# An interaction tower on one core: ScalarE's five banks per job added by GpSimd alone, or by an accumulating DMA and GpSimd

## What is computed

```python
prev = x.transpose(...)                       # [b, e, h], h = 39, then 128, 128
for k in range(3):
    z = einsum('bmd,bhd->bdmh', x, prev)      # 39 fields times h
    t = z.reshape(b, d, m*h) @ ws[k] + bs[k]  # to 128 units
    t = t / sqrt(sum(t*t over units and d))   # a norm per example
    logit.append(t); prev = t
features = sum(concatenate(logit), over d)    # 384 per example
```

## Time and profile before

| | |
|---|---|
| three timed runs | 1060.4, 1061.88, 1062.07 us (median 1061.88) |
| profiled execution | 1062.48 us, its span 1060.8 us |
| PE busy | 1028.2 us (97%) |
| DVE busy | 983.6 us (93%) |
| POOL busy | 865.9 us (82%) |
| ACT busy | 791.3 us (75%) |
| granted TensorE clock | 1.00 throughout |

### The profile page before, as it was taken

One profiled execution on the slowest core, in us unless ns is written; L12 is line 12 of the kernel. 1 busy time (PEld: TensorE's weight loads), 2 busy tenths in 40 slices (PEclk: granted clock), 3 DMA queues, 4 the chain that ended last, 5 costly groups with the idle time before them and its releaser, 6 DMA issues.

```text
span 1060.8 us, 17970 instructions
## 1 busy us (share of the span) xinstructions
PE 1028.2 (97%) x4320; PEld 782.4 (74%) x4320; DVE 983.6 (93%) x3344; ACT 791.3 (75%) x2655; POOL 865.9 (82%) x729
## 2 busy tenths in 40 slices
PE   2999999999999999999999999999999999999998
PEld 0477777878777787877778787777878777788884
DVE  2589999999999999999999999999999999999993
ACT  3476877868788786868778687777868778788872
POOL 6777988889898888988888898888889888577770
PEclk9999999999999999999999999999999999999999
DMA  5650030302303030120303012030301203000000
GB/s 188 129 143 12 3 88 3 89 2 52 96 4 88 3 87 4 21 71 2 89 3 87 5 28 64 3 89 2 85 7 17 74 3 89 1 1 1 2 1 1
DMA packets 75892, 46.10 MB, mean 43 GB/s; under 512 B 55689, under 2 KB 58633, under 8 KB 75658
## 3 DMA queue, kind: packets, MB, share of 16 engines
q1 hardware_dynamic: 68487, 38.59, 15.2%
q10 hardware_dynamic: 2179, 5.07, 1.4%
q0 software_dynamic: 5120, 1.29, 1.4%
HBM read 42.99 MB, written 1.94 MB: 42 GB/s over the span
## 4 chain that ended last, share of the span: by engine, by line
PE 48%; POOL 19%; DVE 18%; issue 9%; ACT 5%; DMA 1%; POOLq 0%; DVEq 0%; SPq 0%; ACTq 0%
POOL sums L432 14%; DVE sums L946 12%; PE acc L778 8%; PE bank_d L722 7%; PE bank_d L723 6%; PE bank_d L724 6%; PE bank_a L724 6%; PE bank_a L722 6%; PE bank_a L723 6%; POOL gathered L415 5%; ACT scaled L560 4%; DVE bank_d L946 2%; DVE sums L965 1%; ACT sums L560 1%; PE turned L799 1%
## 5 line engine op out<-in xcount | busy, mean ns | idle before, releaser
L432 POOL TENSOR_TENSOR sums<-sums,scaled 128x512 f32<-128x512 f32 (+1 forms) x512 | 645.1, 1262 | 133.4 <-ACT scaled L560 97.4
L946 DVE SCALAR_TENSOR_TENSOR sums<-bank_d,x_col,sums 128x128 f32<-128x128 f32 x2304 | 654.2, 339 | 29.3 <-PE bank_d L724 20.2
L560 ACT ACTIVATE scaled<-bank_a,x_col 128x128 f32<-128x128 f32 x1920 | 551.5, 385 | 139.8 <-PE bank_a L724 132.7
L722 PE MATMUL bank_d<-w_hi,prev_lo 128*128 128x512 f32 x640 | 288.0, 450 | 6.2 <-DVE sums L965 4.7
L722 PE MATMUL bank_a<-w_hi,prev_lo 128*128 128x512 f32 (+1 forms) x640 | 263.9, 412 | 2.6 <-issue 1.3
L724 PE MATMUL bank_d<-w_hi,prev_hi 128*128 128x512 f32 x640 | 252.5, 394 | 0.0
L723 PE MATMUL bank_d<-w_lo,prev_hi 128*128 128x512 f32 x640 | 252.1, 394 | 0.0
L724 PE MATMUL bank_a<-w_hi,prev_hi 128*128 128x512 f32 (+1 forms) x640 | 245.3, 383 | 0.0
L723 PE MATMUL bank_a<-w_lo,prev_hi 128*128 128x512 f32 (+1 forms) x640 | 245.1, 383 | 0.0
L560 ACT ACTIVATE sums<-bank_a,x_col 128x128 f32<-128x128 f32 x512 | 146.1, 369 | 76.8 <-PE bank_a L724 75.9
L415 POOL DMA_INDIRECT gathered<-in_table,idx x160 | 177.2, 1108 | 28.5 <-issue 18.3
(11 more groups left out here) (84 smaller groups left out, 528.2 us busy)
## 6 DMA issues: line engine op xcount, KB each, us to landing
x_pairs<-x_scratch SPq DMA_DIRECT2D x135, 156.0 KB
x_pairs<-x_scratch SPq DMA_DIRECT2D x96, 78.0 KB
gathered<-in_table,idx POOLq DMA_INDIRECT x160
x_sq<-x_scratch SPq DMA_DIRECT2D x32, 64.0 KB
x_pairs<-x_scratch SPq DMA_DIRECT2D x92, 22.0 KB
x_scratch<-gathered SPq DMA_DIRECT2D x16, 72.0 KB
w_raw<-in_w ACTq DMA_DIRECT2D x1, 1024.0 KB, 5.1
w_raw<-in_w ACTq DMA_DIRECT2D x1, 896.0 KB
```

The costliest lines, as they stand in the source:

```text
L432: nc.gpsimd.tensor_tensor(out=sums[:, n % SUMS, 0:w, :], in0=sums[:, n % SUMS, 0:w, :], in1=scaled[:, a - 1, 0:w, :], op=ALU.add).then_inc ...
L560: op = nc.scalar.activation(to[:, i, :], bank_a[at % A_RING][:, i * UNITS:(i + 1) * UNITS], ACT.Copy, scale=x_of(c, q, a * PER_BANK + i))
L722: nc.tensor.matmul(to, lo, w_h, start=True, stop=False)
L946: nc.vector.scalar_tensor_tensor(out=taken(n, u) if u in LEFT else total, in0=taken(n, u), scalar=x_of(c, q, A_FIELDS + u), in1=total, op0 ...
```

## The change

In jobs 11 to 116 ("far" jobs) one DMA, issued by GpSimd with an addition, adds `scaled` buffers 3 and 4 to buffers 1 and 2; GpSimd then adds only these two to `sums`. Its two additions stand four and five banks behind bank 4 of their job. There are two sets of `scaled` buffers now, by the job's parity (the second lies in space of `w_raw` that is no longer used from job 11 on). The lead of the A banks grows from 7 to 12 in jobs 5 to 9 (six A banks each) and falls back in jobs 116 to 120 (four each). In the far jobs the gathers stand at slots 3 and 4 instead of 1 and 2. The core of the diff (`scale_bank`'s waits, the order of the slots on ACT and PE, and DVE's wait for `added_all(n)` follow the same tables):

```diff
-LEAD = 7
+LEAD, FAR_LEAD = 7, 12
+FAR_FROM, FAR_TO = 11, NJ - 12
+LEADS = [min(max(LEAD, LEAD + n - 5), FAR_LEAD, max(LEAD, FAR_LEAD + FAR_TO - n)) for n in range(NJ + 1)]
+FAR_ADDS = {1: A_BANKS - 1, 2: A_BANKS}
+def a_first(n):
+    return A_BANKS * n + LEADS[n]
+def a_count(n):
+    return a_first(n + 1) - a_first(n) if n + 1 < NJ else A_BANKS
+ADDS_BEHIND = {at: [] for at in range(A_BANKS * NJ)}
+for _n in range(NJ):
+    for _a in range(1, A_BANKS):
+        if not is_far(_n):
+            ADDS_BEHIND[A_BANKS * _n + _a].append((_n, _a))
+        elif _a in FAR_ADDS:
+            ADDS_BEHIND[A_BANKS * _n + A_BANKS - 1 + FAR_ADDS[_a]].append((_n, _a))
...
+        def pair_of(n, a):
+            first = scaled[:, a - 1:a + 1, :, :] if n % 2 == 0 else scaled_odd[(a - 1) // 2][:, :, :, :]
+            return first.rearrange("p a i u -> p (a i u)")[:, 0:(PER_BANK + a_fields_of(A_BANKS - 1)) * UNITS]
...
-            def add_bank(at):
+            def add_banks(at):
                 n, a = divmod(at, A_BANKS)
-                pool.wait_ge(a_scaled, at + 1)
-                if a > 1:
-                    pool.wait_ge(a_added, ADDS * n + a - 1)
-                w = a_fields_of(a)
-                nc.gpsimd.tensor_tensor(out=sums[:, n % SUMS, 0:w, :], in0=sums[:, n % SUMS, 0:w, :],
-                                        in1=scaled[:, a - 1, 0:w, :], op=ALU.add).then_inc(a_added, 1)
+                if is_far(n) and a == A_BANKS - 1:
+                    pool.wait_ge(a_scaled, at + 1)
+                    nc.gpsimd.dma_start(pair_of(n, 1), pair_of(n, 3), accum_op=ALU.add).then_inc(pair_added[n % 2], 16)
+                for n, a in ADDS_BEHIND[at]:
+                    if is_far(n):
+                        pool.wait_ge(pair_added[n % 2], pairs_added_by(n))
+                    else:
+                        pool.wait_ge(a_scaled, at + 1)
+                    if a > 1:
+                        pool.wait_ge(a_added, ADDED[n, a - 1])
+                    w = PER_BANK if is_far(n) else a_fields_of(a)
+                    nc.gpsimd.tensor_tensor(out=sums[:, n % SUMS, 0:w, :], in0=sums[:, n % SUMS, 0:w, :],
+                                            in1=scaled_of(n, a)[:, 0:w, :], op=ALU.add).then_inc(a_added, 1)
...
-                for a in range(A_BANKS):
-                    add_bank(A_BANKS * n + LEAD + a)
-                    if 1 <= a <= per_step and first + a - 1 < GATHERS:
-                        gather(it + 2, first + a - 1)
+                begin = 1 if n < FAR_FROM else 3
+                for a in range(max(a_count(n), A_BANKS)):
+                    if a < a_count(n):
+                        add_banks(a_first(n) + a)
+                    if begin <= a < begin + per_step and first + a - begin < GATHERS:
+                        gather(it + 2, first + a - begin)
```

More of the change, by code:

```diff
@@ L67, with is_far, added_all @@
 JOB_AT = {j: n for n, j in enumerate(JOBS)}
+FAR_FROM, FAR_TO = 11, NJ - 12
+LEADS = [min(max(LEAD, LEAD + n - 5), FAR_LEAD, max(LEAD, FAR_LEAD + FAR_TO - n)) for n in range(NJ + 1)]
+FAR_ADDS = {1: A_BANKS - 1, 2: A_BANKS}
+def is_far(n):
+    return FAR_FROM <= n <= FAR_TO
+def a_first(n):
[9 more added lines that the diff above has]
+            ADDS_BEHIND[A_BANKS * _n + A_BANKS - 1 + FAR_ADDS[_a]].append((_n, _a))
+ADDED = {}
+for _at in range(A_BANKS * NJ):
+    for _add in ADDS_BEHIND[_at]:
+        ADDED[_add] = len(ADDED) + 1
+def added_all(n):
+    return ADDED[n, max(FAR_ADDS) if is_far(n) else A_BANKS - 1]
 def step_at(it, q):
@@ L200, in cin_kernel @@
         identity = sb("identity", [128, 128])
-        w_raw = {k: sb(f"w{k}_raw", [128, FIELDS, UNITS]) for k in (1, 2)}
+        used = 28
+        with ExitStack() as first_life:
+            w_raw = {k: first_life.enter_context(nc.sbuf_tensor(f"w{k}_raw", [128, FIELDS, UNITS], f32)) for k in (1, 2)}
+        scaled_odd = []
+        for k in (1, 2):
+            sb(f"raw_rows{k}", [128, used, UNITS])
+            scaled_odd.append(sb(f"scaled_odd{k}", [128, 2, PER_BANK, UNITS]))
+            sb(f"raw_rest{k}", [128, FIELDS - used - 2 * PER_BANK, UNITS])
         w_hi = {k: sb(f"w{k}_hi", [128, FIELDS, UNITS], f32r) for k in (1, 2)}
@@ L285, in cin_kernel @@
         a_added = sem("a_added")
+        pair_added = [sem(f"pair_added{parity}") for parity in range(2)]
         d_ready = sem("d_ready")
@@ L323, in cin_kernel, with scaled_of, pairs_added_by @@
         TOP_LOADS = 2 * 3 + 2
+        def scaled_of(n, a):
+            if n < FAR_FROM or n % 2 == 0:
+                return scaled[:, a - 1, :, :]
+            return scaled_odd[(a - 1) // 2][:, (a - 1) % 2, :, :]
+        def pair_of(n, a):
+            first = scaled[:, a - 1:a + 1, :, :] if n % 2 == 0 else scaled_odd[(a - 1) // 2][:, :, :, :]
+            return first.rearrange("p a i u -> p (a i u)")[:, 0:(PER_BANK + a_fields_of(A_BANKS - 1)) * UNITS]
+        def pairs_added_by(n):
+            return 16 * ((n - FAR_FROM) // 2 + 1)
         def a_fields_of(a):
@@ L464, in _ @@
                 gather(2, j)
-            for at in range(LEAD):
-                add_bank(at)
+            for at in range(LEADS[0]):
+                add_banks(at)
             for n in range(NJ):
@@ L555, in scale_bank @@
                 else:
-                    if n >= 1:
-                        act.wait_ge(a_added, ADDS * (n - 1) + a)
-                    to = scaled[:, a - 1, :, :]
+                    was = n - 1 if n < FAR_FROM else n - 2
+                    if n == FAR_FROM:
+                        act.wait_ge(w_lo_made[1], len(W_PIECES[1]))
+                        act.wait_ge(w_lo_made[2], len(W_PIECES[2]))
+                    elif is_far(was) and a > max(FAR_ADDS):
+                        act.wait_ge(pair_added[was % 2], pairs_added_by(was))
+                    elif was >= 0:
+                        act.wait_ge(a_added, ADDED[was, a] if (was, a) in ADDED else added_all(was))
+                    to = scaled_of(n, a)
                 for i in range(a_fields_of(a)):
@@ L668, in _ @@
                                  ACT.Copy).then_inc(prev_hi_made[1], 1)
-            for at in range(LEAD):
+            for at in range(LEADS[0]):
                 scale_bank(at)
-                if at == LEAD - 2:
+                if at == LEADS[0] - 2:
                     square_x(1)
             for n in range(NJ):
-                for a in range(A_BANKS):
-                    scale_bank(A_BANKS * n + LEAD + a)
+                for a in range(max(a_count(n), A_BANKS)):
+                    if a < a_count(n):
+                        scale_bank(a_first(n) + a)
                     if (n, a) in W2_HIGH_AT:
@@ L836, in _ @@
                     else:
-                        bank_for_act(A_BANKS * n + LEAD + a)
-                        a += 1
+                        until = a + 1 if place < len(PATTERN) - 1 else a_count(n)
+                        while a < until:
+                            bank_for_act(a_first(n) + a)
+                            a += 1
                     if place == 5 and n:
@@ L938, in add_field @@
                 if u < PER_BANK:
[L939 removed]
+                    dve.wait_ge(a_added, added_all(n))
                 elif u < D_FIELDS - 1:
```

6 lines of the change are left out of this document (2 added, 4 removed).

## The result

The changed kernel took 1072.4 us (median of 4 runs, 1071.0 to 1077.5) against 1062.0 us: ratio 1.011, 95% interval 1.008 to 1.014. It is slower by 1.1%; the forecast was 0.5% faster. The time lies inside the stated range of 1047 to 1074 us, on the other side of the kernel before. The profiled execution is the longest of the four, with a span of 1075.8 us against 1060.8; of its 15 us some 5 are its own.

What follows compares the result with a forecast made beforehand. PE sets the pace (61.9 of 62.25 us per chunk), DVE close behind. Terms -0.87 -0.16 +0.55 +0.05 = -0.43 us per chunk, 13 chunks -5.6, took 1062.5 to 1056.9; forecast 1056.5, range 1047 to 1074.

Steps and rivals of the forecast that it cites:

- the landing: Accumulating DMA from issue to landing: 4.8 us, 5.5 to 6 beside the pair loads in jobs 50 and 51; +0.05 us per chunk.
- landing too slow: Rival: landing over 5.4 us makes GpSimd's round longer than a short job; jobs 50, 51 lose, +1.2 per chunk, 1078; chance 0.13.
- Step 0: Job 52, a chunk's first multiply: 1.5 us in place of 2.19, with the prev_lo wait, empties PE's stall, -0.87 us per chunk.
- about as it is: DVE's wait for GpSimd's last addition (at 448.12, 0.31 us behind GpSimd) stays nearly unchanged under the new queue order.
- Step 2: Job 54: a chunk's third multiply comes free at 1.21 us and PE's stall goes, -0.16 us per chunk.
- caught: Rival: third multiply held behind issue and addition, 3.3 us; job 54 +0.7 in place of -0.16 per chunk, 1067.5; chance 0.18.
- The wait for prev_lo: Job 49, fourth A slot: PE stalls for prev_lo of the next chunk, once per chunk, +0.55 us.
- The ramp: Lead of 12: jobs 5 to 9 bring 3.5 us of PE forward, jobs 116 to 120 return it; costed 0, up to 2.
- The sum itself: Per chunk -0.43 us, 13 chunks -5.6, from 1062.5 to 1056.9; median 0.6 lower, forecast written as 1056.5.
- GpSimd's issue: GpSimd's time to issue one accumulating DMA of 128 partitions: 1.0 us, from 0.5 to 1.8.

Runs made afterwards that it cites:

- tiny_loads: The changed kernel with each of SyncE's pair loads fetching 128 bytes of a row in place of 2048 from chunk 2 on: 1060.8 us, ratio to before 0.999.
- tiny_dma: The changed kernel with each accumulating DMA adding 512 bytes of a row in place of 3584, the rest never added: 1066.9 us, ratio to before 1.004.
- mixed: The changed kernel without the transfer in jobs of steps 0 and 1, where GpSimd adds all four banks: 1056.9 us, ratio to before 0.996.
- others_out: The changed kernel without the transfer in jobs of steps 3 and 4, where GpSimd adds all four banks: 1096.2 us, ratio to before 1.031.

## Why the prediction was wrong

The step that failed is the landing: "there I expect 5.5 to 6 and GpSimd at most half a microsecond late. PE doesn't feel that at once", costed at 0.05 us a chunk. Measured: 5.8 to 8.5 us for step 0's job and 4.5 to 9.3 for step 1's. tiny_loads prices it: ratio 0.999 against 1.011, 1.3% or 13 us in all, with chunk 4's late pair tiles in it. The rival "landing too slow" had the mechanism, its place (jobs 50 and 51) and nearly its size, 1.2 us a chunk or 15.6 in all. How it is spread it didn't have: against tiny_loads, step 0's jobs are 0.7 us longer in the mean of twelve chunks and 5.9 us in chunk 4, which it didn't name.

By its terms, in the profiled execution (sum over chunks 2 to 14, job times after less before):

- Step 0, forecast -0.87 a chunk (-11.3). Measured -1.1 us for the 12 chunks without the fourth, and +5.7 in the fourth. The gain itself was right in size where no landing disturbs: -0.78 in tiny_dma, -0.73 in mixed. What failed is "GpSimd is now in its wait for the DMA ... or in the one addition after it": in chunks 6 to 9, 11 and 13 a landing of 6.2 to 6.5 us ends that wait just as the multiply comes, so it is caught (2.1 to 2.3 us against the 1.5 taken). In chunks 2, 3, 5, 10 and 12, with landings of 6.5 to 8.0 us, it is free, but DVE then waits 1.2 to 1.9 us for GpSimd's additions, and these jobs are the longer ones (9.5 to 10.3 us against 9.1 to 9.4). The prediction had put DVE's wait "about as it is".
- Step 2, forecast -0.16. Right for 8 chunks; in the other 5 the rival "caught" came true, +0.9 each, +4.5. It was put at 0.7 for all 13 or none; who came first changed from chunk to chunk with the landing.
- The wait for prev_lo, forecast +0.55. It is there, in the job named, 13 times: 7.54 less 7.19, +0.35 each, +4.6. Right in kind. The 0.35 us taken for the semaphore and a weight load were too much: from the end of prev_lo to the start of the matmul it is 0.05 us in the trace, and that matmul takes 0.51 us in place of 0.39.
- The ramp, put at 0, "up to 2". Chunk 1 +4.4, chunk 15 -2.05: +2.3 net, and 2.0 to 2.9 in the variants with the same ramp (mixed +4.4 and -2.35). The five banks are PE's own 3.5 us where PE sets the pace; at the end DVE's lag, and step 6 (7.74 against 7.07), keep a part of them.
- Step 6 gained 0.09 a chunk, which wasn't foreseen.
- The sum itself has a slip: 1056.9 less 0.6 is 1056.3, not 1056.5, which changes nothing.
- GpSimd's issue (forecast 1.0) is 0.93 us, the landing without other loads (4.8) is 4.3. The second addition after an issue takes 1.67 us, so the additions sum to 431 us, not 390.

Together +11.8 in chunks 2 to 14, +2.3 for the ramp and +0.9 at the start are the 15 us of the two spans. The start differs by as much and more between executions of kernels that are equal there (chunk 1 began at 83.8 to 90.2), so that term is none of the change.

An issue by itself holds nothing: in mixed the second multiply starts 0.45 us behind one with no addition behind it and takes 1.22 us. Multiplies caught 0.3 to 0.6 us behind an issue end 1.09 us behind the addition that follows it, and others_out's ended 1.09 us behind the last of four. The Trainium skill (SBUF — State Buffer, Who interferes with whom) has such a multiply and a GpSimd instruction that reads SBUF contend for one port, and the traces agree. Who of the two has it isn't read off the starts in the trace, though: with an addition begun 0.20 us earlier the multiply took 2.45 us in chunk 4 (284.70) and 1.21 in chunk 5 (359.25).

The landing without other loads is 4.3 us, against 3.7 for a plain one of the same size. The Trainium skill (Collectives: The Full Stack, The bandwidth ceiling) has transfers that add slower by a factor of nearly two; the prediction's estimate by it was 4.8 to 5, and the trace is below that.

What stays open: the own cost of three gathers a step, and a run that takes DVE's two extra instructions out of chunk 5's first steps: that they make its jobs long is read from the trace, not tried. A version without the wait for prev_lo, which by 13 times 0.35 would give some 4 us more (an estimate), wasn't found.
